# Q, K, V and output projections: one fp32 matmul each in place of three fp16 matmuls of high and low halves

## What is computed

```python
mod = (silu(c) @ wmod).reshape(B, 6, 1, -1)          # sa, ca, ga, sb, cb, gb per batch
h = layernorm(x) * (1 + ca) + sa
Q, K, V = (einsum('bsd,ed->bse', h, W) for W in (W_Q, W_K, W_V))   # split into 16 heads of 8
Q, K = rope(Q), rope(K)
attn = softmax(causal(Q K^T / sqrt(8)))
x = x + ga * einsum('bsd,ed->bse', attn V, W_O)
h = layernorm(x) * (1 + cb) + sb
xn = rmsnorm(h) * ln_w;  logits = xn @ Wg + bg;  top 2 of 8, softmax of the two
x = x + gb * sum_e w_e * ((silu(xn W1a_e + b1a_e) * (xn W1b_e + b1b_e)) @ W2_e + b2_e)
```

## Time and profile before

| | |
|---|---|
| median of 3 runs | 671.4 us (671.26 to 672.26) |
| span of the profiled execution, first to last instruction | 669.5 us |
| what lies around that span, against the median | 1.9 us |
| TensorE busy | 575.0 us, 86% of the span |
| VectorE busy | 464.9 us, 69% |
| ScalarE busy | 428.4 us, 64% |
| GpSimd busy | 342.2 us, 51% |
| chain of work that ended last, share on TensorE | 80% |

### The profile page before, as it was taken

The page is one execution under the profiler, slowest core; times in us unless marked ns, Lnnn a source line. Parts: engine busy times, 40 slices in busy tenths (PEclk is TensorE's granted clock), DMA queues, the critical chain, the costliest instruction groups (busy, mean ns, idle before and its releaser), DMA issues.

```text
span 669.5 us, 19952 instructions
## 1 busy us (share of the span) xinstructions
PE 575.0 (86%) x5529; PEld 419.3 (63%) x5530; DVE 464.9 (69%) x1571; ACT 428.4 (64%) x1108; POOL 342.2 (51%) x501
## 2 busy tenths in 40 slices
PE   3599999999999999999999998218999999999700
PEld 1366666666666666666666665107888888888600
DVE  5665677787778768768767663454777777777646
ACT  3457665766767757766667655116888888888700
POOL 5432254565665655656656444650545545555553
PEclk9989999999999999999999999657999999999955
DMA  8212011112112112101212102132121211111066
GB/s 240 60 56 57 10 48 41 40 54 68 32 52 63 48 35 59 55 30 57 55 34 55 47 19 62 50 97 59 55 61 50 61 56 49 55 54 52 27 181 196
DMA packets 53668, 41.53 MB, mean 62 GB/s; under 512 B 7554, under 2 KB 48341, under 8 KB 53616
## 3 DMA queue, kind: packets, MB, share of 16 engines
q1 hardware_dynamic: 43056, 29.12, 16.4%
q0 software_dynamic: 4544, 8.54, 3.6%
q10 hardware_dynamic: 6016, 3.24, 1.6%
HBM read 24.80 MB, written 12.78 MB: 56 GB/s over the span
## 4 chain that ended last, share of the span: by engine, by line
PE 80%; DVE 7%; DMA 4%; issue 3%; ACT 2%; POOL 2%; SPq 0%; DVEq 0%; ACTq 0%; POOLq 0%
PE bank L1162 15%; PE bank L1126 8%; PE bank L1163 6%; PE bank L1319 5%; PE bank L1321 5%; PE bank L1320 5%; PE bank L1150 4%; PE bank L1139 4%; PE bank L1138 3%; PE bank L1340 3%; PE bank L1341 3%; PE bank L1114 3%; PE bank L1342 2%; PE bank L1175 2%; PE bank L1151 2%
## 5 line engine op out<-in xcount | busy, mean ns | idle before, releaser
L796 DVE TENSOR_REDUCE nmax<-bank 128x3 f32<-128x384 f32 x256 | 140.6, 555 | 75.5 <-PE bank L1126 71.1
L601 ACT ACTIVATE probs<-bank 128x384 f32<-128x384 f32 x256 | 126.7, 495 | 45.2 <-PE bank L1126 42.5
L1126 PE MATMUL bank<-cb,c 128*128 128x256 bf16 x512 | 140.6, 275 | 0.0
L554 POOL DMA_INDIRECT expert_outs<-y_sb,number_of x78 | 78.7, 1010 | 92.7 <-ACT y_sb L704 78.7
L1162 PE MATMUL bank<-probs,v_aug 128*32 128x256 f32 x512 | 119.1, 391 | 0.0
L1036 DVE SCALAR_TENSOR_TENSOR h<-bank,b_sb,silu_a 128x256 f32<-128x256 f32 x156 | 71.6, 479 | 51.4 <-ACT silu_a L715 51.2
L1319 PE MATMUL bank<-xt,we_hi 128*128 128x256 f16 x312 | 86.3, 277 | 1.9 <-ACT xt L689 0.8
L1320 PE MATMUL bank<-xt,we_hi 128*128 128x256 f16 x312 | 86.1, 276 | 0.0
L1321 PE MATMUL bank<-xt,we_lo 128*128 128x256 f16 x312 | 86.1, 276 | 0.0
L695 ACT ACTIVATE hh<-h 128x256 f16<-128x256 f32 x156 | 64.2, 411 | 19.1 <-DVE h L1036 14.4
L468 POOL DMA_INDIRECT expert_rows<-send,pos_i x64 | 63.3, 990 | 25.3 <-issue 12.2
(11 more groups left out here) (179 smaller groups left out, 1354.5 us busy)
## 6 DMA issues: line engine op xcount, KB each, us to landing
g_in<-expert_rows SPq DMA_DIRECT2D x39, 132.0 KB
k_pad<-qk_t SPq DMA_DIRECT2D x128, 32.0 KB, 1.9
mod_b<-mod_rows SPq DMA_DIRECT2D x16, 256.0 KB, 3.2
we_lo<-expert_outs SPq DMA_DIRECT2D x16, 256.0 KB, 3.9
wstage<-in_L_ffn_W1a_dram SPq DMA_DIRECT2D x16, 128.0 KB, 2.2
wstage<-in_L_ffn_W1b_dram SPq DMA_DIRECT2D x16, 128.0 KB, 2.3
wstage<-in_L_ffn_W_dram SPq DMA_DIRECT2D x16, 128.0 KB, 2.4
out_dram<-we_lo ACTq DMA_DIRECT2D x16, 128.0 KB, 3.5
```

The source lines that it names most:

```text
L554: pool.indirect_dma_start(out=outs, out_offset=bass.IndirectOffsetOnAxis(ap=number_of[:, r, s:s + 1], axis=0), in_=y_sb[:, r, s, :], in_of ...
L601: nc.scalar.activation(probs[:, k % 4], col_bank[k % 2][:, 0:S + P], ACT.Exp, scale=SM_SCALE).then_inc(probs_ready, 1)
L796: nc.vector.tensor_reduce(nmax[:, k], row_bank[k % 2][:, 0:3 * P].rearrange("p (c t) -> p c t", t=P), AX.X, ALU.max, negate=True).then_inc ...
L1126: return mm(diagonal, ident16, mask.unsqueeze(1).broadcast_to([P, 2, P]), start=False, stop=True, skip_group_check=True)
```

## The change

`w_hi` and `w_lo` become one fp32 tile `w_t`, `ht_hi` and `ht_lo` are gone and `ht32` is used itself, `on_hi` and `on_lo` become one fp32 tile `on_sb`. Each call of `halves` becomes one matmul with fp32 operands. The instructions that made the halves are gone: ScalarE's second modulation (L644) and GpSimd's subtraction (L475) for each batch, VectorE's `on_lo` (L814) for each batch, and VectorE's `w_lo` (L955) once. The waits move accordingly: the projection waits for `h32` in place of `h_lo`, the output projection for `on_sb` in place of `on_lo`, the first projection for the weight copy on ScalarE in place of VectorE's fourth set-up step.

```diff
-        w_hi = sb("w_hi", [P, 4, D], F16)
-        w_lo = sb("w_lo", [P, 4, D], F16)
+        w_t = sb("w_t", [P, 4, D])
...
-        ht_hi = sb("ht_hi", [P, S], F16)
-        ht_lo = sb("ht_lo", [P, S], F16)
...
-        on_hi = sb("on_hi", [P, S], F16)
-        on_lo = sb("on_lo", [P, S], F16)
+        on_sb = sb("on_sb", [P, S])
...
                 if s0:
-                    pool.wait_ge(act0.sem, act0.after(b0, "h_hi"))
-                    nc.gpsimd.tensor_tensor(ht_lo[:], ht32[:], ht_hi[:], ALU.subtract).then_inc(pool0.sem, 1)
-
                     if due(pe1.after(plus(b0, -2), "tb")):
...
-            nc.scalar.activation(w_hi[:], banks[2][:].rearrange("p (n d) -> p n d", d=D), ACT.Copy).then_inc(setup_act.sem, 1)
+            nc.scalar.activation(w_t[:], banks[2][:].rearrange("p (n d) -> p n d", d=D), ACT.Copy).then_inc(setup_act.sem, 1)
...
-                        nc.scalar.activation(on_hi[:], tail_bank[:, 0:S], ACT.Copy).then_inc(act3a.sem, 1)
+                        nc.scalar.activation(on_sb[:], tail_bank[:, 0:S], ACT.Copy).then_inc(act3a.sem, 1)
...
-                            nc.scalar.activation(ht_hi[:], chain_a[:, 0:S], ACT.Identity, scale=scale_in[:, at], bias=shift_in[:, at]).then_inc(act0.sem, 1)
...
-            def low_out(b):
-                vec.wait_ge(act3a.sem, act3a.after(b, "on_hi"))
-                nc.vector.tensor_tensor(on_lo[:], tail_bank[:, 0:S], on_hi[:], ALU.subtract).then_inc(vec3a.sem, 1)
...
-                        if k == 11:
-                            low_out(ba)
...
-                vec.wait_ge(setup_act.sem, 2)
-                nc.vector.tensor_tensor(w_lo[:], banks[2][:].rearrange("p (n d) -> p n d", d=D), w_hi[:], ALU.subtract).then_inc(setup_vec.sem, 1)
...
-            def halves(o, l_hi, l_lo, r_hi, r_lo, start=True, stop=True):
-                mm(o, l_hi, r_hi, start=start, stop=False, skip_group_check=True)
-                mm(o, l_hi, r_lo, start=False, stop=False, skip_group_check=True)
-                return mm(o, l_lo, r_hi, start=False, stop=stop, skip_group_check=True)
...
-                halves(o, ht_hi[:, at], ht_lo[:, at], w_hi[:, 0:3, :].rearrange("p n d -> p (n d)"), w_lo[:, 0:3, :].rearrange("p n d -> p (n d)")).then_inc(pe0.sem, 1)
+                mm(o, ht32[:, at], w_t[:, 0:3, :].rearrange("p n d -> p (n d)"), start=True, stop=True, skip_group_check=True).then_inc(pe0.sem, 1)
...
-                            pe.wait_ge(vec3a.sem, vec3a.after(ba, "on_lo"))
+                            pe.wait_ge(act3a.sem, act3a.after(ba, "on_sb"))
                             for s in range(NS):
                                 at = slice(P * s, P * s + P)
-                                t = halves(tail_bank[:, at], on_hi[:, at], on_lo[:, at], w_hi[:, 3], w_lo[:, 3], start=(s == 0))
+                                t = mm(tail_bank[:, at], on_sb[:, at], w_t[:, 3], start=(s == 0), stop=True, skip_group_check=True)
...
-                                pe.wait_ge(setup_vec.sem, 4)
-                            pe.wait_ge(pool0.sem, pool0.after(b0, "h_lo"))
+                                pe.wait_ge(setup_act.sem, 2)
+                            pe.wait_ge(act0.sem, act0.after(b0, "h32"))
```

More of the change, by code:

```diff
@@ L234, in build @@
         setup_pe = steps("setup_pe", "c_t w_t mod_t b1_t")
-        setup_act = steps("setup_act", "silu w_hi b1")
-        setup_vec = steps("setup_vec", "scale shift copied w_lo abs_a abs_b sign_a sign_b sgn_a sgn_b gate_a gate_b plus1")
+        setup_act = steps("setup_act", "silu w_t b1")
+        setup_vec = steps("setup_vec", "scale shift copied abs_a abs_b sign_a sign_b sgn_a sgn_b gate_a gate_b plus1")
         wstage_in = [sem("wstage_in0"), sem("wstage_in1")]
@@ L243, in build @@
         vec0 = steps("vec0", "cos0 sin0a sin0b cos1 sin1a sin1b hi0 hi1")
-        act0 = steps("act0", "h32 h_hi v0 v1 khi0 khi1 ev0 ev1_keys ev1 w_hi")
-        pool0 = steps("pool0", "h_lo zero_m turn0 turn1 qlo0 klo0 qlo1 klo1 w_lo")
+        act0 = steps("act0", "h32 v0 v1 khi0 khi1 ev0 ev1_keys ev1 w_hi")
+        pool0 = steps("pool0", "zero_m turn0 turn1 qlo0 klo0 qlo1 klo1 w_lo")
         rows_ready, max_ready = sem("rows_ready"), sem("max_ready")
@@ L251, in build @@
         pe3a = steps("pe3a", "o0 o1 on_t wo")
-        vec3a = steps("vec3a", "rs0 on0 rs1 on1 on_lo gated")
-        act3a = steps("act3a", "on_hi")
+        vec3a = steps("vec3a", "rs0 on0 rs1 on1 gated")
+        act3a = steps("act3a", "on_sb")
         pool3a = steps("pool3a", "resid")
@@ L953, in set_up @@
                 nc.vector.tensor_copy(mod_sb[:], banks[3][0:B, :]).then_inc(setup_vec.sem, 1)
-                vec.wait_ge(setup_act.sem, 2)
-                nc.vector.tensor_tensor(w_lo[:], banks[2][:].rearrange("p (n d) -> p n d", d=D), w_hi[:], ALU.subtract).then_inc(setup_vec.sem, 1)
                 gate = mod_sb[:].rearrange("p (g d) -> p g d", d=D)
-                vec.wait_ge(setup_vec.sem, 4)
+                vec.wait_ge(setup_vec.sem, 3)
                 for n, g in ((0, 0), (1, 3)):
                     nc.vector.tensor_scalar(square[0:B, n, :], gate[:, g], -1.0, None, ALU.mult).then_inc(setup_vec.sem, 1)
-                vec.wait_ge(setup_vec.sem, 6)
+                vec.wait_ge(setup_vec.sem, 5)
                 for n, g in ((0, 0), (1, 3)):
@@ L965, in set_up @@
                     nc.vector.tensor_scalar(h_s[0:B, n, :], gate[:, g], 0.0, 2.0, ALU.is_ge, ALU.mult).then_inc(setup_vec.sem, 1)
-                vec.wait_ge(setup_vec.sem, 10)
+                vec.wait_ge(setup_vec.sem, 9)
                 for n, g in ((0, 0), (1, 3)):
```

## The result

The changed kernel takes 680.49 us (median of four runs, 679.22 to 683.12) against 671.83 us for the kernel before on the same chip: +8.7 us, or 1.3% by these medians. The ratio used for comparison, which isn't the quotient of the two medians, is 1.014 with a 95% interval of 1.0112 to 1.0168. The forecast was 679.7 us, +8.3.

The account below looks back on a forecast made before the run. TensorE was taken to bound the attention stage. Projections +7.0, output projection +1.5, start-up -0.3 and last batch +0.1 sum to +8.3 us, 671.4 to 679.7 us (range 675.8 to 684).

Parts of the forecast that it names:

- TensorE sets the period, and its turns are paid in full: Attention stage: TensorE fills 24.17 of 24.26 us, others have slack; what the change adds to TensorE is paid once a batch.
- the stated sign of being wrong: Wrong if the step after the load isn't 0.32 us a record, or the period doesn't grow by what TensorE's turns grow.
- Four passes, two records, 0.32 us a record: Q, K, V projections: an fp32 column costs four fp16 columns, two records a matmul, 0.64 us for 384 columns.
- half rate: Rival: matmul lowered to half the passes, projection 0.43 us in place of 0.75; total -1.4, 670.0 us; chance 0.03.
- The first load is open: Projections behind the values: first fp32 load of 0.11 us not hidden, 0.50 to 0.75 us each; 28 x 0.25 = +7.0 us.
- The rival of the hidden load: First fp32 load of a projection hidden under the matmul before, +0.14 each; total +5.1, 676.5 us; chance 0.15.
- The output projection, 0.44 us bound by the load: Six fp16 matmuls taking 0.34 us become four fp32 records of 0.11 us each, 0.44 us: +0.10 us a batch.
- The count of 15: Output projection: fifteen of sixteen batches count, 15 x 0.10 = +1.5 us.
- The freed work is worth nothing: Work removed from ScalarE, GpSimd and VectorE lies under work waiting for TensorE: 0 from batch 2 on.
- Start-up, -0.3: Batch 0 gains 0.4 us from the earlier projection, batch 1 loses 0.1: together -0.3 us (-1.2 to +0.5).
- the place of the lower clock: The rest: a clock that falls for a few us at another place of the start-up; chance 0.03.
- The sum for loads that never overlap, 689.5: Rival: fp32 loads never overlap, 10.1 + 8.0 + 0.1 = +18, 689.5 us; partly or wholly open loads, chance 0.12.

Follow-up runs that it names:

- first pair: The original profiles of the kernel before and the changed kernel, whose medians were 671.83 and 680.49 us.
- experiment 4: Changed kernel, but TensorE issues the projection at heads 3 and 5 before the values, right behind the mask matmul: 676.2 us, ratio 1.009 to the kernel before.
- experiment 2: Kernel before with only the output projection in fp32, Q, K and V still in fp16 halves: 673.02 us, ratio 1.0044.
- second profile of the kernel before: Kernel before run and profiled once more with no edit: 671.99 us, period 24.10 us.
- 9: Changed kernel with values of heads 2 and 3 of each group of four issued together, and unread halves still made and waited for: 634.07 us, ratio 0.9475.
- experiment 3: Changed kernel with ht_hi, ht_lo and on_lo still made and waited for, though nothing reads them: 680.03 us, ratio 1.0146 to the kernel before.
- second profile of the changed kernel: Changed kernel run and profiled once more with no edit: 678.8 us, period 24.70 us.
- second pair: Both kernels profiled once more with no edit: 671.99 us for the kernel before, 678.8 us for the changed one.
- experiment 7: Kernel before with the values of heads 2 and 3 of each group of four issued together: 627.61 us, ratio 0.9347.

## Why the prediction was right

*TensorE sets the period, and its turns are paid in full.* Right. Against the undisturbed 24.10 us the period grew by 0.60, forecast 0.6. In the earlier trace rows the period was 24.26, with 0.16 of late signals in it that I took for part of the program, so the forecast period of 24.9 didn't come (24.70), and the first pair of profiles alone (+0.44) met the stated sign of being wrong, a period that doesn't grow by TensorE's turns. The 1.7 us of waits that I counted left out the row of the weight load shown above (3.4 us), in which this hold-up stood.

*Four passes, two records, 0.32 us a record.* Right: 64 records for 32 projections, 0.75 us from start to start, of which 0.11 is the first load and 0.64 the columns. This decides the question between the Trainium skill's half rate ("Perfetto Trace Analysis", Engine Utilization) and its four passes ("FP8 and Floating Point Precision", TensorE Precision Notes) for four: half the rate is what each of the two records shows (0.32 us against 0.16 for an fp16 matmul), and the whole matmul takes both.

*The first load is open.* Right, shown by the steps of 0.43 and 0.32 us of its two records and by experiment 4: -0.19 us a period when it is taken from behind the values. The rival of the hidden load would have had 0.64 in the trace.

*The output projection, 0.44 us bound by the load.* 0.45. The columns of a record (0.107 us) and its load (0.11) are too close to tell which of them sets the steps of 0.112. The count of 15 was too high: between the modulations of batches 3 and 15 experiment 2 loses 1.2 us to the second profile of the kernel before, which is eleven output projections, and behind batch 15 nothing. The changed kernel loses 0.5 us behind it, its two projections, so the last output projections are covered by other waits.

*The freed work is worth nothing.* Right for the period, by experiments 3 and 9. In the start-up it is worth 1.3 us (experiment 3), which the prediction had there, against longer projections.

*Start-up, -0.3.* Right in its part and wrong as a sum: the first projection began at 12.0 in place of 12.15 and the second V came at 14.94 (forecast 15.1), and the modulation of batch 2 came 0.51 us earlier (0.84 between the second profiles). Two profiles have no 3.4 us of the lower clock in their start-up, that of experiment 2, whose start-up is the kernel before's but for one more small copy, and the second of the changed kernel: there the modulation of batch 2 comes at 39.29 and 39.02, which is the -0.3. What the prediction gave a chance of 0.03 and no price is the place of the lower clock, which moves later stretches by 1.1 to 1.3 us from execution to execution of one kernel. The sum for loads that never overlap, 689.5, leaves out the -0.3.

*Sum.* 8.3 forecast, 8.7 measured as a difference of medians; the profiled spans differ by 10.0 in the first pair and 6.2 in the second (670.1 and 676.3). Taken apart by the starts of the modulations and of the last scatter (us, after less before):

| | first pair | second pair |
|---|---|---|
| to batch 2 | -0.51 | -0.84 |
| batch 2 to 3 | +1.55 | -0.85 |
| batch 3 to 15 | +5.57 | +7.16 |
| batch 15 to the last scatter | +0.46 | +0.43 |
| behind the last scatter | +2.99 | +0.25 |

Batch 3 to 15 is 12 times 0.60 in the second pair; the first lacks 1.6 of it by the late signals in the profile before. Batch 2 to 3 is the place of the lower clock; with the full clock in it (21.45 against 21.19) the change costs 0.3. Of the 3.0 behind the last scatter, where the change touches nothing, 1.4 lies ahead of the expert stage, where a transfer landed after 5.70 us in place of 4.47, and for 1.6 no cause is known. So what the profiles show of the change itself is -0.3 + 0.3 + 7.2 + 0.5 = 7.7 us of the 8.3 forecast; the missing 0.6 is mostly the output projections that were counted and are covered. The close agreement of 679.7 with 680.5 is in part luck: one profile pair alone could have shown 6 or 10.

## What to carry to other kernels

Count an fp32 matmul as four fp16 ones in columns and as two weight loads of 0.11 us; replacing three fp16 matmuls of halves by it frees other engines but adds a third to TensorE's columns. Where TensorE sets the period that is a loss, even with the 0.45 us of waits in experiment 7. That it would pay where TensorE has more slack isn't shown by a run here; only the start-up hints at it, where the freed work is worth 1.3 us. Look at the distance from start to start behind each neighbour, since the same load is free after a long matmul of the same shape and open after a change of shape. And before explaining 0.1 us a period or 1 us of start-up by an edit, profile the unchanged kernel twice, and read the waits of the weight loads beside those of the matmuls.

## What the runs showed of the hardware that I had not expected

- Two engines can start about 1 us behind the work of TensorE that they wait for, at the same place of eight loop passes, in one execution and not in the next of the same program (ScalarE 0.96 us after the transposes against 0.03). None of the other eleven profiles of this case has more than 0.2 us there.
- A stretch of 3.4 us at the lower TensorE level starts at 33.4 us in one execution, at 38 in another and is absent from a third (second profile of the changed kernel). In the 3 us ahead of the fall TensorE is busy for 1.7 us (33.4) and 1.5 us (38.7 and 38.3); in the profile without a fall it is busy for 1.6 and 1.5 us in the same places.
- Two fp32 matmuls of 32 stationary columns side by side cost as much as one (0.45 us to the next for 256 moving columns, either way), with the 0.09 us at the change of shape counted once. Pairing all of them was worth 44 us, five times what the change cost.
